# A query rest projection one period earlier, a query rotary unit one period later, behind the values

## What is computed

```python
B, S, D = x.shape            # 32 samples, 256 tokens, 128
xn = layernorm(x)
qkv = einsum('bsm,qhdm->bqhsd', xn, W_qkv)          # 16 heads of 64
qk = qkv[:, :2, :, :, :rope_dim]                    # rope_dim = 32
qk_rot = qk * cos + rotate_half(qk) * sin
qkv = qkv.at[:, :2, :, :, :rope_dim].set(qk_rot)
scores = where(causal, -inf, Q @ K.T) / 8
attn = softmax(scores) @ V @ W_o
x = x + attn + experts(xn)                          # top 2 of 8 experts and a skip gate
```

## Time and profile before

| | us |
|---|---|
| median of 3 runs | 1347.32 (1346.56 to 1348.73) |
| the profiled execution | 1345.19 |
| its span | 1343.4 |
| former half, first scores of sample 1 to those of sample 15 | 141.5 to 570.8 |
| latter half, first scores of sample 17 to those of sample 31 | 875.7 to 1303.6 |

### The profile page before, as it was taken

The page is one execution under the profiler, slowest core; times in us unless marked ns, Lnnn a source line. Parts: engine busy times, 40 slices in busy tenths (PEclk is TensorE's granted clock), DMA queues, the critical chain, the costliest instruction groups (busy, mean ns, idle before and its releaser), DMA issues.

```text
span 1343.4 us, 46788 instructions
## 1 busy us (share of the span) xinstructions
PE 1228.7 (91%) x15156; PEld 941.8 (70%) x15157; DVE 1075.4 (80%) x3911; ACT 1108.1 (82%) x3608; POOL 956.9 (71%) x1349
## 2 busy tenths in 40 slices
PE   0547999999999999997999999899999999999998
PEld 0524677777777777676899899667777777777766
DVE  5888888888887887775777777888888888888885
ACT  6617889999988888886788788888888888988896
POOL 3115899999999999893222221688888888888885
PEclk9657999999999999998999999999999999999999
DMA  9993443333343343334444443243333343334431
GB/s 289 291 272 88 101 95 82 81 82 82 84 101 92 83 100 96 80 102 130 131 125 129 129 129 107 58 118 91 90 89 90 92 109 99 90 92 109 105 92 31
DMA packets 154040, 149.07 MB, mean 111 GB/s; under 512 B 12784, under 2 KB 113520, under 8 KB 153584
## 3 DMA queue, kind: packets, MB, share of 16 engines
q1 hardware_dynamic: 145264, 129.21, 37.7%
q0 software_dynamic: 8576, 17.33, 4.4%
HBM read 38.28 MB, written 41.09 MB: 59 GB/s over the span
## 4 chain that ended last, share of the span: by engine, by line
PE 52%; POOL 19%; issue 9%; DVE 9%; DMA 6%; SPq 2%; ACT 2%; POOLq 0%; DVEq 0%; ACTq 0%
PE bank L1174 10%; PE bank L1175 9%; PE bank L1176 9%; PE bank L1259 7%; PE bank L1288 6%; PE bank L1248 5%; POOL sorted_x_dram L541 3%; POOL arena L514 3%; PE bank L1272 3%; POOL arena L519 2%; POOL arena L512 2%; POOL arena L497 2%; DMA sorted_x_dram<-stage,slots 2%; POOL arena L498 2%; PE bank L1289 2%
## 5 line engine op out<-in xcount | busy, mean ns | idle before, releaser
L714 ACT ACTIVATE probs<-arena,neg_max 128x128 f32<-128x128 f32 (+1 forms) x1024 | 452.9, 448 | 76.5 <-DVE neg_max L1027 68.2
L1027 DVE CUSTOM_DVE_ANT_0 arena<-bank,causal 128x128 f32<-128x128 f32 (+1 forms) x1024 | 303.1, 351 | 35.1 <-PE bank L1248 34.4
L1259 PE MATMUL bank<-ident,probs 128*128 128x128 f32 x1536 | 212.1, 274 | 5.7 <-ACT probsT L696 5.1
L1259 PEld LDWEIGHTS bank<-ident,probs 128*128 128x128 f32 x1536 | 177.9, 142 | 28.1 <-issue 5.6
L714 ACT ACTIVATION_READ_ACCUMULATOR probs<-arena,neg_max 128x1 f32 x1024 | 197.4, 193 | 0.0
L514 POOL TENSOR_TENSOR arena<-o_whole,arena 128x256 f16<-128x256 f32 x256 | 172.6, 674 | 21.1
L1174 PE MATMUL bank<-arena 128*128 (+1 forms) x864 | 183.7, 239 | 1.8 <-DVE arena L1148 1.7
L1175 PE MATMUL bank<-arena 128*128 (+1 forms) x864 | 184.8, 239 | 0.0
L1248 PE MATMUL bank<-arena 64*128 64x128 f16 (+1 forms) x3072 | 172.7, 246 | 9.8 <-DVE neg_max L1027 5.2
L1176 PE MATMUL bank<-arena 128*128 (+1 forms) x864 | 180.7, 238 | 0.0
L560 POOL TENSOR_TENSOR arena<-arena 128x256 f32<-128x256 f32 x72 | 55.7, 773 | 166.1 <-DMA arena<-sorted_x_dram 166.0
(11 more groups left out here) (154 smaller groups left out, 3211.7 us busy)
## 6 DMA issues: line engine op xcount, KB each, us to landing
arena<-arena SPq DMA_DIRECT2D x256, 256.0 KB, 3.6
arena<-sorted_x_dram SPq DMA_DIRECT2D x144, 128.0 KB, 2.2
sorted_x_dram<-stage SPq DMA_DIRECT2D x6, 2304.0 KB, 17.8
sorted_y_dram<-stage SPq DMA_DIRECT2D x72, 128.0 KB, 1.8
sorted_x_dram<-stage SPq DMA_DIRECT2D x2, 2368.0 KB, 19.1
arena<-experts_dram SPq DMA_DIRECT2D x8, 512.0 KB, 6.3
out_dram<-acc SPq DMA_DIRECT2D x32, 128.0 KB
sorted_x_dram<-stage,slots POOLq DMA_INDIRECT x128
```

Source lines behind the costliest of these rows:

```text
L714: last = nc.scalar.activation(probs[:, s % 4, at:at + w], masked[:, s % 4, at:at + w], ACT.Exp, bias=neg_max[:, s % 4, t:t + 1], scale=-1. ...
L1027: last = nc.vector.tensor_tensor_reduce(out=masked[:, (s + i) % 4, at:at + w], in0=SC[i][:, at:at + w], in1=causal[:, 2 * P - w:2 * P], sc ...
L1259: last = nc.tensor.transpose(TP[s % 2][:, k * P:(k + 1) * P], probs[:, s % 4, k * P:(k + 1) * P], ident[:])
```

## The change

In AHEAD, rest 1 moves from period 7 to period 6 and rope 0 from period 6 to period 7. In period 6 the two units are now the low values 0 and then rest 1 (before: rope 0 and then the values); in period 7 they are the low values 1 and then rope 0 (before: the values and then rest 1). Everything that follows a unit by the rules above moves with it. The change acts in samples 0 to 14 and 16 to 29, those that have a sample two further on to work for (with 14 working for 16). In the last sample of each half, and in the one before the last, 30, nothing is moved.

```diff
-AHEAD = ((5, "rest", 0), (6, "rope", 0), (7, "rest", 1))
+AHEAD = ((5, "rest", 0), (6, "rest", 1), (7, "rope", 0))
...
-    steps = [(p, kind, j, b + 2) for p, kind, j in AHEAD if further and kind == "rope"]
-    steps += [(p, kind, j, b if kind == "v_high" else b + 1)
+    steps = [(p, kind, j, b if kind == "v_high" else b + 1)
               for p, kind, j in (OPENERS if opening else USUAL) if nearer or kind == "v_high"]
...
     steps += [(p, kind, j, b + 1) for p, kind, j in VALUES if nearer]
-    steps += [(p, kind, j, b + 2) for p, kind, j in AHEAD if further and kind == "rest"]
+    steps += [(p, kind, j, b + 2) for p, kind, j in AHEAD if further]
```

## The result

The changed kernel takes 1349.84 us (median of 20 runs, 1346.96 to 1353.69), the kernel before 1346.82 (20 runs beside them, 1344.73 to 1351.25). The ratio is 1.0022, with a 95% interval from 1.0013 to 1.0031. The forecast was 1338.0 us, and both its time and its sign were wrong. The profiled execution of the changed kernel has a span of 1347.4 us against 1343.4.

What follows compares the result with a forecast made beforehand. TensorE's own work was taken as the floor (30.15 us a sample), with GpSimd setting the former half's pace. Gains of 8.9 us (latter half) and 0.4 (former) made 9.3, giving 1338.0 us, range 1333 to 1343.

Steps and rivals of the forecast that it cites:

- Period 0's wait gone: Latter half, period 0: TensorE's 0.45 us wait for rest_low and VectorE's 1.5 us idle ahead of it disappear.
- So I take all of 0.57 as gone in a steady latter sample: Latter half: TensorE's whole 0.57 us of waiting per steady sample goes, 12 x 0.57 = 6.8 us.
- the 8.9 us: Latter half's total gain: 6.8 steady samples, 0.3 sample 18, 1.2 start of 17, 0.6 rest 2 of 17.
- The lower bound, 0.3: Latter half: if the least slack, 0.2 us, is used up and costs as much again, 0.3 us per sample is left.
- Rival D: All engines shift together and the latter half's waits return at other places: 1347 us, chance 0.07.
- rival B: Period 7 or 0: TensorE waits for the values copy or rope 0's bank, halving the gain: about 1342.5, chance 0.15.
- The start of 17, 1.2 us: Start of sample 17: 1.2 of TensorE's 1.46 us wait for the stacked keys goes, rope_low 3 coming earlier.
- Rest 2 of sample 17, 0.6 us: Sample 17: the same DMAs release rest_high 2 sooner, so TensorE's wait for it goes, 0.6 us.
- GpSimd's order changes, not its work: Former half: GpSimd stays the pace at 30.55 us per sample, so only 0.4 us is gained in all.
- the slack of 0.2 us at rope_add 0: Former half: GpSimd reaches rope_add 0 at 446.1, turn 0 is done at 445.9, so no wait, by 0.2 us.
- rival C: Former half: turn 0 comes too late and GpSimd starves; slower, 1355 us at 1.4 us late, chance 0.06.
- and a loss, priced below: Former half's bound on the downside: every tenth that turn 0 is late for GpSimd costs 1.4 us over 14 samples.

Runs made afterwards that it cites:

- e3: Changed kernel with GpSimd's mix of the next sample moved from period 2 into period 7, ahead of rope_add 0, in the latter half: 1342.12 us, ratio 0.9959.
- e12: Changed kernel with rope_low 0 on VectorE instead of GpSimd in samples 1 to 15 and 17 to 31: 1336.82 us.
- e13: The changed kernel itself, run once more: 1349.39 us, ratio 1.002.
- e2: Changed kernel with the old order kept in samples 0 to 15, the new one only in the latter half: 1345.43 us, ratio 0.9993.
- e15: Changed kernel with the last send of samples 1 to 15 into a third buffer that the experts don't read: 1345.82 us, ratio 0.9992.
- e11: The kernel of e6 run again (kernel before, GpSimd's mix in period 7 in the latter half): 1344.12 us, ratio 0.998.
- e6: Kernel before, with GpSimd's mix of the next sample moved from period 2 into period 7 in the latter half: 1357.46 us.
- e4: Changed kernel with rope_low 0 of samples 1 to 15 on VectorE instead of GpSimd: 1338.70 us, ratio 0.994.

## Why the forecast was wrong

- **Period 0's wait gone:** right. TensorE's wait for rest_low in period 0 and VectorE's 1.5 us of idle time are not in the trace any more.
- **"So I take all of 0.57 as gone in a steady latter sample":** wrong, and the largest error. It measured 0.07, so 12 x 0.5 = 6 of the 8.9 us did not come. (Of the twelve samples only 11 were steady: sample 30 took 29.08 us before, and fell by 0.45.) Rest 1's own followers and rope 0's bank were checked, and rightly but for 0.1 us. Not followed was GpSimd: the change takes rope_low 0 (1.16 us) from ahead of its wait for turn 1 to behind it. The forecast stopped at the split after rope_add 0. The overlap that the forecast counted on was missing there: five periods on, ScalarE waits 1.09 us for GpSimd, and rest_low 0 with it, which had 0.15 us to spare ahead of period 6's second unit in the forecast's rows of the former half, makes that unit 0.29 us late. e3 and e12 take work from GpSimd there and the 0.57 comes. The lower bound, 0.3 from "the least slack, 0.2", was too high for the same reason: a wait was bounded by slacks of the wrong queue. Rival D, that the latter waits return at other places (0.07), describes the latter half best; rival B named the values copy and rope 0's bank, which cost at most 0.1 us each.
- **The start of 17, 1.2 us:** mostly right. The wait of 1.46 is now 0.51, and 0.48 and 0.52 in e13 and e2:

```profile
879.76 0.67 PE L1247 MATMUL bank<-arena 64*128 64x128 f16 x12 [0.51 <-issue]
885.87 0.28 PE L1173 MATMUL bank<-xnT_lo,wqk_hi 128*128 128x256 f16 x1 [0.62 <-DVE arena L987]
```

- **Rest 2 of sample 17, 0.6 us:** wrong in this execution, by the second of these rows: 0.45 before, 0.62 now. But it is 0.28 in e2, which has the same new order there, and gone in e13, the same kernel. In each ScalarE's rounding of rest 2 waits for a stacking DMA, as forecast, 1.25 us before, 1.47 here, 1.12 in e2 and 0.95 in e13, so the mechanism holds and the landing varies. Samples 16 and 17 together took 62.69 us before, 62.57 in this execution, 61.52 in e2 and 61.47 in e13: of the 1.8 us forecast for both terms, 1.2 came in those two. Samples 20, 27 and 29 are 0.15 to 0.8 us longer than before, and in e13 sample 24 by 1.4, so that the half as a whole gained nothing.
- **The former half, "GpSimd's order changes, not its work":** the pace and the slack of 0.2 us at rope_add 0 were right, steady samples stayed at 30.55 to 30.6, and rival C's mechanism did not happen. The step that failed is that only rope_add's wait was examined, and the sends' waits were put at nothing ("and a loss, priced below" was priced for a late turn only). rope_add 0 had been the spacing between two sends of the same buffer; taken out from between them, the second caught up with the first one's landing. Price: 3.3 us by the profile, 3.6 by e13 and e15, where the forecast had a gain of 0.4.
- **Chance:** slower had 0.06, and by another mechanism. That was too sure: each half rested on a bound that was worked out from one queue.

## What to carry to other kernels

When a step is moved on an engine that has no idle time, follow that engine's queue until it idles, here five periods on, and not only to the moved step's next reader. A step that does nothing for a transfer can still be what keeps two transfers apart; look what stood between a send and the one that reuses its buffer. And a reordering that measures as nothing may be half of a gain: with 0.9 and 1.2 us a sample of GpSimd's work put elsewhere, the same change went from +0.2% to -1%, while each of the two reliefs alone brought the old order 0.1 and 0.2%.

## What the runs showed of the hardware

- An indirect send of 128 rows of 512 bytes landed after 2.3 us beside idle DMA engines, and after 3.7 to 5.7 us beside the 256 KB stacking transfers (samples 3 and 4, both kernels; 6.3 in sample 14 of the changed one). In every trace a send that waited over 1 us for a landing started 0.76 to 0.78 us behind the last one recorded, but for the send of period 7 in sample 4 (1.07).
- A semaphore update behind TensorE's scores arrived 0.2 to 1.1 us after their end in some executions, and practically never in others of the same program. The changed kernel shows no difference in time (1349.8 and 1349.4), another 1% (1344.1 in e11 and 1357.5 in e6).
- GpSimd's busy share told nothing of its limit: 28.0 of 30.6 us in sample 10, and yet 1.2 us of its work taken away (e4) brought the sample to 30.14 in the new order.
